# GpSimd multiplies two FFN units in one instruction, and ScalarE copies unit 11 ahead of the router's exponentials

## The reference

```
x = x + conv(ln_c(x))           # q, k, v = silu(t @ W), q and k of unit length; per head, along the 256 tokens:
                                #   u_t = beta_t * (v_t - S^T k_t);  S += k_t u_t^T;  o_t = S^T q_t
                                # then t + o @ Wo
t = tokens(x);  n = ln_t(t)
gates = top 2 of softmax(n @ router_w) of 8 experts, normalized
routed = sum_e gates[e] * ((silu(n @ w_gate[e]) * (n @ w_up[e])) @ w_down[e])
shared = (silu(n @ ws_gate) * (n @ ws_up)) @ ws_down
alpha = sigmoid(n @ sg_w + sg_b)
x = t + alpha * shared + (1 - alpha) * routed
```

## Time and profile before

| | before |
|---|---|
| time, median of three runs | 482.74 us (482.66 to 483.06) |
| the profiled execution, its own time | 483.11 us |
| its span, first to last instruction | 481.4 us |
| granted TensorE clock, mean of the span | 0.947 |
| busy share of PE, DVE, ACT, POOL | 86, 88, 72, 84% |
| largest group of POOL: products of line 1007 | 192 instructions, 112.8 us, 606 ns each |

### The profile page before, as it was taken

The page is one execution under the profiler, slowest core; times in us unless marked ns, Lnnn a source line. Parts: engine busy times, 40 slices in busy tenths (PEclk is TensorE's granted clock), DMA queues, the critical chain, the costliest instruction groups (busy, mean ns, idle before and its releaser), DMA issues.

```text
span 481.4 us, 10362 instructions
## 1 busy us (share of the span) xinstructions
PE 415.3 (86%) x2400; PEld 384.0 (80%) x2400; DVE 421.3 (88%) x2270; ACT 344.5 (72%) x997; POOL 406.0 (84%) x519
## 2 busy tenths in 40 slices
PE   1344446999999999999999999999999989899996
PEld 0233325898999989998999999999999979798895
DVE  4689969999999999999999999999999999996200
ACT  3699546586978786877878686969695847475862
POOL 4366978899999999999999999999999999986340
PEclk9976555999999999999999999999999999999999
DMA  6555672623242223222232322322323232200301
GB/s 164 161 124 131 155 184 73 167 73 98 66 109 81 91 68 89 73 87 78 81 89 72 98 77 84 93 82 81 89 75 90 78 95 84 90 1 1 115 2 16
DMA packets 43437, 42.91 MB, mean 89 GB/s; under 512 B 20144, under 2 KB 35184, under 8 KB 43376
## 3 DMA queue, kind: packets, MB, share of 16 engines
q1 hardware_dynamic: 42768, 42.05, 32.5%
q10 hardware_dynamic: 608, 0.21, 0.2%
HBM read 35.95 MB, written 6.29 MB: 88 GB/s over the span
## 4 chain that ended last, share of the span: by engine, by line
DVE 60%; POOL 10%; PE 10%; issue 7%; ACT 1%; POOLq 0%; DVEq 0%; ACTq 0%
DVE Pr L1423 13%; DVE bank L1427 13%; DVE u L1425 12%; DVE SH L1431 11%; POOL PQ L969 3%; POOL PQ L962 3%; PE bank L463 2%; POOL hid L1007 2%; DVE otok L1236 1%; PE bank L436 1%; PE bank L448 1%; DVE ss L1204 1%; PE bank L440 1%; PE bank L438 1%; PE bank L439 1%
## 5 line engine op out<-in xcount | busy, mean ns | idle before, releaser
L1007 POOL TENSOR_TENSOR hid<-sg,ug 128x192 f32<-128x192 f32 x192 | 112.8, 606 | 22.0 <-ACT ug L714 18.4
L962 POOL TENSOR_TENSOR PQ<-SH,QB 128x768 f32<-128x768 f32 x62 | 112.6, 1838 | 0.7 <-DVE SH L1431 0.7
L713 ACT ACTIVATE sg<-bank 128x192 f32<-128x192 f32 x192 | 64.3, 335 | 61.5 <-PE bank L440 48.7
L969 POOL TENSOR_TENSOR PQ<-PQ 128x768 f32<-128x768 f32 (+2 forms) x93 | 102.9, 1106 | 6.1
L463 PE MATMUL bank<-Wd,hidT 128*128 128x192 f32 x576 | 106.6, 326 | 0.0
L1427 DVE TENSOR_TENSOR bank<-bank,u 128x96 f32<-128x96 f32 (+1 forms) x467 | 104.5, 265 | 0.5
L1425 DVE TENSOR_REDUCE u<-Pr 128x6 f32<-128x102 f32 (+1 forms) x437 | 102.5, 268 | 0.8 <-issue 0.3
L1423 DVE TENSOR_TENSOR Pr<-SH,bank 128x96 f32<-128x96 f32 (+1 forms) x437 | 101.0, 265 | 1.4
L1431 DVE TENSOR_TENSOR SH<-SH,bank 128x96 f32<-128x96 f32 (+1 forms) x467 | 101.9, 255 | 0.3
L463 PEld LDWEIGHTS bank<-Wd,hidT 128*128 128x128 f32 x576 | 94.4, 190 | 0.0
L436 PE MATMUL bank<-Whi,hiT 128*128 128x384 f32 (+1 forms) x192 | 73.0, 380 | 1.1 <-DVE loT L1166 1.1
(11 more groups left out here) (143 smaller groups left out, 814.2 us busy)
## 6 DMA issues: line engine op xcount, KB each, us to landing
QB<-q_scratch SPq DMA_DIRECT2D x64, 384.0 KB
k_scratch<-khl SPq DMA_DIRECT2D x64, 48.0 KB, 1.7
KR<-k_scratch SPq DMA_DIRECT2D x32, 96.0 KB, 2.4
q_scratch<-qn SPq DMA_DIRECT2D x64, 24.0 KB, 1.9
Wd<-in_L_ffn_w_down_dram SPq DMA_DIRECT2D x4, 288.0 KB, 8.2
out_dram<-xT SPq DMA_DIRECT2D x1, 896.0 KB, 4.1
Wlo_unsplit<-in_L_ffn_w_gate_dram SPq DMA_DIRECT2D x2, 384.0 KB, 4.4
Wlo_unsplit<-in_L_ffn_w_up_dram SPq DMA_DIRECT2D x2, 384.0 KB, 5.9
```

The source lines that it names most:

```text
L962: tt(PQ[:, at * BR * HP:(at + n) * BR * HP].rearrange("p (i b h) d -> p i b (h d)", i=n, b=BR), SH[:, lo:lo + n].rearrange("p i b h d -> p ...
L969: chained(tt(PQ[:, :, 0:w], PQ[:, :, 0:w], PQ[:, :, w:2 * w], ALU.add))
L1007: tt(hid[:, r * H:(r + 1) * H], sg[:, m % RING], ug[:, m % RING], ALU.mult).then_inc(s_hid, 1)
```

## The change

GpSimd's `hidden` takes two neighbouring units, m and m + 1, in one instruction of 384 columns. It waits for both units' copies and for the turn that frees both places in `hid`, and counts two on its semaphore. GpSimd's order names only the even units: the pair 6-7 stands behind rsqrt, 8-9 behind the first half's products, 10-11 behind the sums and the key normalization, and 0-1, 2-3 and 4-5 of the next block behind the normalization of v. Before, unit 6 stood ahead of rsqrt, units 8, 9 and 10 stood together ahead of the sums, and unit 0 stood ahead of the second half's products. ScalarE copies unit 11 right behind hidden 1, ahead of Fc_out and the table load for the exponentials. TensorE's, VectorE's and the DMAs' programs stay as they are.

```diff
                     at(-2, hidden, 1)
+                    at(-2, unit, 11)
                     at(-3, Fc_out)
                     table(c + 2, LN_EXP)
                     at(2, A_inv)
...
                     table(0, SILU)
                     at(-2, hidden, 2)
-                    at(-2, unit, 11)
                     at(-1, unit, 0)
...
             def hidden(q, p, m):
-                pool.wait_ge(s_ug, q * UN + (m + 1))
+                pool.wait_ge(s_ug, q * UN + (m + 2))
 
                 if m >= UN // 2 or later(q, 1):
-                    last = ((m - UN // 2) % UN + 1) * H - 1
+                    last = ((m + 1 - UN // 2) % UN + 1) * H - 1
                     g = [lo * P <= last < hi * P for lo, hi in GRP].index(True)
                     pool.wait_ge(s_ht, q * NG + (g + 1 - (0 if m >= UN // 2 else NG)))
-                r = m % (UN // 2)
-                tt(hid[:, r * H:(r + 1) * H], sg[:, m % RING], ug[:, m % RING], ALU.mult).then_inc(s_hid, 1)
+                r, s = m % (UN // 2), m % RING
+                tt(hid[:, r * H:(r + 2) * H].rearrange("p (m h) -> p m h", m=2), sg[:, s:s + 2], ug[:, s:s + 2],
+                   ALU.mult).then_inc(s_hid, 2)
...
                     once(c, 1, weights_1, 9)
-                    at(-2, hidden, 6)
                     if c <= NC:
                         rsqrt(c)
-                    at(-2, hidden, 7)
+                    at(-2, hidden, 6)
                     once(c, 1, weights_1, 10)
                     once(c, 1, weights_1, 11)
                     at(0, reading, 0)
                     at(-2, hidden, 8)
-                    at(-2, hidden, 9)
-                    at(-2, hidden, 10)
                     at(0, summing, 0)
                     at(2, A_kn)
-                    at(-2, hidden, 11)
+                    at(-2, hidden, 10)
                     at(2, A_qn)
-                    at(-1, hidden, 0)
                     at(0, reading, 1)
                     at(0, summing, 1)
                     at(2, A_vn)
-                    at(-1, hidden, 1)
+                    at(-1, hidden, 0)
                     at(-1, hidden, 2)
-                    at(-1, hidden, 3)
                     at(-1, hidden, 4)
-                    at(-1, hidden, 5)
                     at(2, A_klo)
```

## The result

The changed kernel takes **535.2 us** (median; its executions lie between 531.5 and 538.3), the kernel before 482.8 us beside it: a ratio of 1.108, interval 1.104 to 1.111. It is slower, in the place and by the mechanism that the main sum named, but 23 us beyond its 512 and 5 us above the upper end of its range. The profiled execution took 538.26 us with a span of 536.5, 55.1 more than before. Chunk 15 begins on VectorE at 460.70 us where it began at 409.96: 50.7 of the 55.1 lie in the loop, the rest in the tail.

A forecast was written before the change was run, and what follows sets the result against it. VectorE's serial chain was taken as the bound, 25.2 us per chunk. A delay of 2.1 us in 13 chunks, 27.3, plus 1.9 in the tail, 29.2 together, on 483.11 gave 512.3, against the median 512; range 504 to 530.

The forecast's parts named there:

- main sum: Loop and tail: late Fb_turn 3 makes VectorE wait 2.1 us in 13 chunks; 29.2 us in all, 506 to 525, chance 0.62.
- What bounds it: Loop: VectorE's serial chain of small products and sums sets the pace, about 25.2 us per chunk.
- 3 per cent of air: TensorE in the loop: its small idle share, cited for the delay being partly taken up, 490 to 505, chance 0.08.
- Part 1: GpSimd's paired products: 1.00 us per pair, 0.86 to 1.21; the saving on GpSimd is worth nought.
- Part 2: Pair 10-11 behind sums and key normalization: Fb_turn 3 starts 2.43 us later, chunks take some 27.3 us.
- Part 3: ScalarE's unit 11 ahead of the exponentials: 0.53 us later copies, 0.1 us per chunk alone, nought in the change.
- Cost nought here: Unit 11 early in the changed kernel: Fb_turn 3's wait for GpSimd until 259.24 covers the 0.53 us.
- Part 4: Ring of four buffers: unit 4's copy waits for pair 0-1; nought taken, up to 0.3 us per chunk kept.
- the chance of 0.25 for the clock: TensorE's pause ahead of Fb_turn 3: chance 0.25 that its clock falls in about half the chunks or more.
- Against it that TensorE is otherwise dense: TensorE in the loop: its dense work outside the some 3 us pause, argued against the clock falling.
- the rival: TensorE's clock falls at the pause: 1.9 us each, six to thirteen falls, 11 to 25 us, 523 to 537; chance 0.25.

The follow-up runs named there:

- run 6: Kernel before with only ScalarE's copy of unit 11 moved ahead of the router's exponentials, single products in their old order; 487.5 us, ratio 1.010.
- run 5: Changed kernel with pair 10-11 put ahead of the first half's sums and six u and gate buffers instead of four; 489.7 us, ratio 1.015.
- run 2: Changed kernel with fourteen unused TensorE products run in the pause ahead of Fb_turn 3, and six u and gate buffers instead of four; 514.3 us, ratio 1.065.
- run 1: Changed kernel with fourteen unused TensorE products run in the pause ahead of Fb_turn 3, still four buffers; 521.9 us, ratio 1.081.
- run 7: Changed kernel with six u and gate buffers instead of four, nothing else altered; 532.1 us, ratio 1.096.
- run 10: Kernel before, with GpSimd instead of VectorE making the two negated mean products of the normalisations behind rsqrt; 488.6 us, ratio 1.011.
- Run 4: Changed kernel with only pair 10-11 moved ahead of the sums, behind pair 8-9, still four buffers; 525.1 us, ratio 1.088.
- run 3: Changed kernel with single products in place of pairs, in the pairs' order, unit 11 still copied early; 523.2 us, ratio 1.084.

## Why the prediction was wrong, step by step

The parts, by undoing the change one step at a time:

| from | to | what is between | us |
|---|---|---|---|
| before, 482.8 | run 6, 487.5 | unit 11 early | 4.7 |
| run 6 | run 5, 489.7 | pairs, 10-11 early, six buffers | 2.1 |
| run 5 | run 2, 514.3 | pair 10-11 behind sums and A_kn | 24.7 |
| run 2 | run 1, 521.9 | ring of four | 7.6 |
| run 1 | changed, 535.2 | the clock's falls | 13.3 |

Runs 1 and 2 hold the fourteen products, which do not delay the turn. The shares depend on which is undone first. By way of run 7 the ring is worth 3.1 and the clock 17.8, together the same 20.9; and unit 11's 4.7 is its price in the kernel before, not behind a late pair.

Three lines of the kernel before bear on the points below: TensorE's largest wait from 85 to 434 us, a stretch in the start (columns as in the earlier trace rows), and TensorE's first instruction behind it.

```profile
PE bank L448 <- ACT hidT L724: 7.0, 12, 0.7
...
27.30:30.60 3.30, 0.80 (x4) 0.38 (x3) 2.73 (x14) 3.21 (x9) 2.19 (x3) 1.00 0.42 106
...
32.02 0.69 PE L403 MATMUL bank<-KR,Sel 128*128 128x384 f32 x1 [3.56 <-DVE SH L1431]
```

- **What bounds it** was half right. VectorE without a wait was read as VectorE alone setting the pace. Run 6 shows a second way round of nearly the same length, over turn 3 and hidT (25.21 us against 25.17), and run 10 a third over GpSimd (25.05). The second is visible before: TensorE's idle time in the earlier trace rows, 302.40 less 293.63, is 8.8 us, and most of it is the wait of the first line above. "3 per cent of air" lay for the most part in that wait; it stands ahead of the turn, for a copy that is itself on the way round, and was no reserve against a later copy.
- **Part 1** held: 1006 ns against 1.00 us, and GpSimd's relief was worth nought in the loop (25.76 us per chunk in run 5, 25.75 in run 6).
- **Part 2** held. Pair 10-11 ends 12.14 us after rsqrt (11.92); most of the difference is pair 6-7, which starts 0.83 us behind rsqrt's start instead of 0.67. With the clock kept up (run 2) VectorE waits 2.1 us per chunk and a chunk takes 27.55 us (27.3).
- **Part 3** was wrong for the move by itself, 0.58 us in most chunks and 0.40 on the mean in place of 0.1 (run 6). "Cost nought here" is argued and not shown: the way over the pair is longer and would cover it, but no run has the late pair with unit 11 in its old place. The step that failed subtracts 0.39 us in every chunk. A reserve in a loop is spent once, and pays again only where a longer chunk has refilled it.
- **Part 4** was mis-sized. Nought was taken and 0.3 per chunk kept: 0.21 per chunk with the clock up, but also 3 to 4 us in chunk 2, where ScalarE waited 5.9 us for pair 0-1 and TensorE 3.35 us for ScalarE. The prediction had laid out no chunk 2; it reasoned from chunk 8.
- **The step that put the time outside the range** is the chance of 0.25 for the clock. The fall was priced: 1.9 us each, six to thirteen of them, 523 to 537. It came in nearly every chunk: without it the time is 521.9 us and inside the range (run 1), while without the ring's part it is still 532.1 and outside (run 7). "Against it that TensorE is otherwise dense" weighed more than the row that showed a fall behind a pause of 2.41 us, shorter than the 3 us forecast. The trace of the kernel before has one more place of the kind, the pause of 3.56 us in the lines above; the clock was 1.00 up to 30.60 and 0.50 from 30.70 on the earlier trace rows, inside that pause. Both places spoke for the rival, though in both TensorE was busy only 0.8 of 3.3 us, and 0.25 was too small a chance. The size of one fall was too large: a chunk of the changed kernel takes 29.0 us on the mean, 1.2 more than in run 1 with the same ring, and with six buffers run 7's 29.0 is 1.5 more than run 2's. In every other chunk some 0.5 us of the stretch of 3.4 us lie in the pause; what else makes it cheaper is not shown.

Run 4 shows besides that the costs are not independent: of the wait at turn 3 1.76 us went away, and 1.74 came back at the buffers.

## What to carry to other kernels

A time in hand that is read in one chunk is a stock: look at it in every chunk of the loop. Where it shrinks from chunk to chunk, a second way round is already as long as the first, and a delay on it is paid in full there. Where a delay opens a pause on TensorE of a length behind which the same trace shows a fall of the clock, take the fall into the main sum. And an engine that is 99 per cent busy in a chain of dependent small instructions is not always relieved by taking an instruction out from between two links: compare the distance of the links with and without one, and look which way round passes through the engine that takes the instruction over.

## What the runs showed of the hardware

- Falls of the clock against the pause ahead of turn 3, as stretches of 3.4 us at half clock beside the turn: at 2.9 to 3.1 us with 12 of 12 turns of the changed kernel and 11 of 12 of run 7; at 2.5 to 2.7 us with five of 12 (run 3); at 2.2 to 2.3 us, at the last two turns of these two kernels, with one of two each time; at 1.2 us with none in runs 4 to 6. The four falls of run 4 past 98 us stand behind its other pause, ahead of L436: two behind pauses of 3.3 and 3.4 us, two behind 1.78, where eight others of 1.7 to 1.9 and one of 2.2 had none. With the pause filled (runs 1 and 2) there was none past 98 us.
- A half-clock stretch of 3.4 us cost 1.2 us (ring of four) or 1.5 us (ring of six) in a loop that waits for TensorE, less than half its length.
- VectorE's busy share counts time that its chain would take without the instruction: 207 ns taken out from between two links, 0.51 us apart, left them 0.52 us apart, and at the second place 0.39 became 0.38. The Trainium skill (Perfetto Trace Analysis, Identifying the Most-Contended Engine) takes the occupancy of VectorE as a fair measure of how near it is to its limit; here it was 99 per cent busy, and two of its instructions per chunk were worth nothing.
